# Two chunks prepared ahead of the loop, three Newton operations on VectorE, and expert weights split beside the last chunk

## The reference, cut to what matters

```
def _layernorm(x): m = mean(x); v = var(x); return (x - m) / sqrt(v + 1e-5)
# layer 0 attention: 16 heads of 8, 120 keys per image from ctx_1024
    q = heads(query @ wq_k + wq_b); k, v = heads(ctx @ wk_k + wk_b), heads(ctx @ wv_k + wv_b)
    attn = softmax(q @ k.T / sqrt(8) + neg) * group_prob
    return (attn @ v) @ wo_k + wo_b
# layer 0 experts: top 2 of 8, each with a capacity; gelu(x @ W1[e] + b1[e]) @ W2[e] + b2[e]
# layer 1 attention: the same without group_prob, one mask for all images
# layer 1 experts: every expert for every row, weighted by comb (zero outside the top 2)
    h = x @ W1[e].T + b1[e]; a, b = split(h); out += ((a * sigmoid(b)) @ Wo.T + bo) * comb[e]
x = x + tanh(g_xattn[0]) * attention0(_layernorm(x), ctx);  x = x + tanh(g_ffn[0]) * experts0(_layernorm(x))
x = x + tanh(g_xattn[1]) * attention1(_layernorm(x), ctx);  x = x + tanh(g_ffn[1]) * experts1(_layernorm(x))
```

## Time and profile before

| | us |
|---|---|
| median of 3 runs | 959.44 (957.41 to 962.17) |
| the profiled execution, its own time | 961.64 |
| its span, first to last instruction | 959.8 |
| PE busy | 793.3 (83%) |
| PEld busy | 627.5 (65%) |
| DVE busy | 670.6 (70%) |
| ACT busy | 608.5 (63%) |
| POOL busy | 571.8 (60%) |

### The profile page before, as it was taken

How to read it: one execution, slowest core, us unless ns; L and a number is a source line. 1 busy time by engine, 2 the same in 40 slices (tenths; PEclk the granted TensorE clock), 3 DMA queues, 4 the chain that set the end, 5 groups by cost and what they waited for, 6 DMA issues and landing times.

```text
span 959.8 us, 20423 instructions
## 1 busy us (share of the span) xinstructions
PE 793.3 (83%) x6554; PEld 627.5 (65%) x6554; DVE 670.6 (70%) x1933; ACT 608.5 (63%) x2582; POOL 571.8 (60%) x872
## 2 busy tenths in 40 slices
PE   2268898988886399999876788788986889999996
PEld 1146666766664299998555556656765767888885
DVE  1246889999896534436688799998896575666664
ACT  1366888998982255444787678889996344444442
POOL 6364567888777500223477887574341767777775
PEclk9978999999996699999999889999998899999998
DMA  7929789536633742322537367454300000000000
GB/s 172 243 87 242 197 218 274 138 98 157 128 86 130 259 138 83 85 82 85 110 85 140 72 127 173 112 109 120 89 13 24 22 23 23 21 15 14 8 12 22
DMA packets 83699, 101.68 MB, mean 106 GB/s; under 512 B 8289, under 2 KB 69926, under 8 KB 82665
## 3 DMA queue, kind: packets, MB, share of 16 engines
q1 hardware_dynamic: 79496, 92.13, 37.4%
q0 software_dynamic: 4096, 8.25, 3.5%
HBM read 63.32 MB, written 45.99 MB: 114 GB/s over the span
## 4 chain that ended last, share of the span: by engine, by line
PE 41%; DVE 22%; ACT 14%; POOL 9%; issue 9%; DMA 5%; SPq 0%; POOLq 0%; ACTq 0%; DVEq 0%
ACT exp L805 10%; PE psum L654 7%; PE psum L691 5%; PE psum L693 5%; PE psum L692 5%; DVE shift L986 5%; DVE exp_T L996 2%; PE psum L542 2%; PE psum L529 2%; PE psum L642 2%; DVE ln_stats L968 2%; PE psum L643 2%; PE psum L644 2%; DVE exp_T L998 2%; PE psum L707 1%
## 5 line engine op out<-in xcount | busy, mean ns | idle before, releaser
L805 ACT ACTIVATE exp<-psum,shift 128x120 f32<-128x120 f32 x1024 | 364.8, 427 | 92.9 <-DVE shift L986 92.5
L805 ACT ACTIVATION_READ_ACCUMULATOR exp<-psum,shift 128x1 f32 x1024 | 269.8, 273 | 0.0
L986 DVE TENSOR_REDUCE shift<-psum 128x4 f32<-128x480 f32 x256 | 164.9, 646 | 55.4 <-PE psum L520 54.8
L529 PE MATMUL psum<-ident,exp 128*120 128x128 f32 x1024 | 164.5, 285 | 35.1 <-DVE exp_T L998 22.0
L1569 POOL TENSOR_TENSOR q_operand<-q_operand 128x512 f32<-128x512 f32 x96 | 125.9, 1311 | 70.3 <-DVE q_operand L1345 66.1
L1345 DVE SCALAR_TENSOR_TENSOR q_operand<-psum,comb,q_operand 128x256 f32<-128x256 f32 x256 | 111.7, 479 | 79.9 <-ACT q_operand L933 79.9
L529 PEld LDWEIGHTS psum<-ident,exp 128*120 128x120 f32 x1024 | 120.4, 143 | 53.9 <-DVE exp_T L998 26.5
L933 ACT ACTIVATE q_operand<-psum 128x512 f32<-128x512 f32 x128 | 76.4, 598 | 122.3 <-PE psum L693 122.2
...
L517 PE MATMUL psum<-neg_rows,const_bf 128*128 128x480 bf16 x256 | 98.7, 386 | 48.4 <-ACT exp L805 27.5
L691 PE MATMUL psum<-w_T_high,xn_T_high 128*128 128x512 f32 x256 | 108.8, 425 | 9.5 <-DVE w_T_low L1311 7.3
L693 PE MATMUL psum<-w_T_high,xn_T_low 128*128 128x512 f32 x256 | 102.5, 400 | 0.0
...
...
## 6 DMA issues: line engine op xcount, KB each, us to landing
...
q_operand<-scratch_q SPq DMA_DIRECT2D x30, 384.0 KB, 6.1
scratch_q<-parts SPq DMA_DIRECT2D x15, 384.0 KB
...
scratch_q<-parts SPq DMA_DIRECT2D x15, 256.0 KB
...
```

The lines of the kernel that those rows point to most:

```text
L529: ins = pe.transpose(ps[0:S2, T_BANKS[G % 2], u * S:(u + 1) * S], atts[l].expS[:, G % RING_E, u, :], ident[:, :])
L805: ins = act.activation(atts[l].expS[:, G % RING_E, u, :], ps[:, S_BANKS[G % 3], u * S2:(u + 1) * S2], ACT.Exp, bias=atts[l].shift[:, i % 2 ...
L986: dve.tensor_reduce(atts[l].shift[:, i % 2, 4 * r:4 * r + 4], ps[:, S_BANKS[G % 3], 0:4 * S2].rearrange("p (h k) -> p h k", h=4), AX_X, AL ...
```

## The change

Three things, in one edit.

**Opening.** Layer 0's chunks 0 and 1 (`READY` = 2) are both prepared ahead of the loop, their splits on VectorE (`split`), their norms too; GpSimd keeps the powers, the clearing of the keys' ring, masks and bias. Rows are loaded chunk by chunk, the spare rows of the queries' ring are cleared ring by ring, and the keys of chunk 0 are fetched before its queries' parts go out. Chunk 2 starts at slot 2 instead of 5.

**Newton on VectorE.** For eight norms (`NEWTON_ON_DVE`) the six operations on GpSimd become three on VectorE (`roots`), placed in the slot of the power, so VectorE awaits the power there. Rows are normalised as (x - mean) * r.

**Second experts' weights.** Their halves lie in two buffers of their own, over rings of keys that are done with: five experts (`v_soon`) once chunk 6's scores are through, three (`v_late`) after the last score. The first split stands at slot 117, the rows' at 115; loads start at slot 60 and come every seven. Units 0 and 1 are multiplied up at slots 130 and 133. To make room, GpSimd's gathers for chunks 5 to 7 and chunk 6's bias work are moved by some slots, and three key splits of layer 1 start three slots later.

```diff
-LAST_AT = 64
+LAST_AT, LAST_EVERY = 60, 7
+
+
+SOON_E = 5
+assert (2 * NCH - 1) % RING == 0
+WEIGHTS_AT = [117 + 2 * e for e in range(SOON_E)] + [129 + e for e in range(E - SOON_E)]
+ROWS_AT = 115
 
 ROUTE_STEPS = 26
...
+NEWTON_ON_DVE = [(0, 0), (0, 1), (0, NCH), (0, NCH + 1), (0, NCH + 2), (0, NCH + 3), (1, NCH - 2), (1, NCH - 1)]
+
+
+def newton_on_dve(who, n):
+
+    return (who, n) in NEWTON_ON_DVE
...
-    return ({1: 0, 2: 5, 3: 14} if l == 0 else {1: 0, 2: 0, 3: 0}).get(P, 16 * P - 38)
+    return ({1: 0, 2: 2} if l == 0 else {1: 0, 2: 0, 3: 0}).get(P, 16 * P - 38)
...
+READY = 2
+
+
+def looped(l, P):
+
+    return l == 1 or P >= READY
-    return ({1: NEAR, 2: MID} if l == 0 else {1: NEAR1, 2: MID1, 3: FAR1, 4: FAR2}).get(P, FAR)
+    return ({2: MID} if l == 0 else {1: NEAR1, 2: MID1, 3: FAR1, 4: FAR2}).get(P, FAR)
-    return {8: 0, 9: 7, 10: 9, 11: 11}[i] if c == 2 else {3: 13, 4: 21, 5: 29, 6: 37, 7: 52}[c] + 2 * b
+    return {8: 0, 9: 7, 10: 9, 11: 11}[i] if c == 2 else {3: 13, 4: 21, 5: 30, 6: 45, 7: 60}[c] + 2 * b
...
+TIGHT6 = dict(TIGHT, exp=18, weigh=21, add_bo=22)
+
+
 def post_at(l, j):
-    return POST if j < 5 else TIGHT if l else TIGHT0
+    return POST if j < 5 else TIGHT0 if l == 0 else TIGHT6 if j == NCH - 2 else TIGHT
-SPLIT_KEYS_AT = {2: (0, 1), 5: (2,), 19: (3, 4, 5)}
+SPLIT_KEYS_AT = {5: (0, 1), 8: (2,), 19: (3, 4, 5)}
...
-        vh, vl = sb(mem, "w1_T_high", [D, E, 2 * HID1], F32R), sb(mem, "w1_T_low", [D, E, 2 * HID1], F32R)
+        v_late = sb(mem, "w1_T_split_late", [D, E - SOON_E, 2, 2 * HID1], F32R)
+        gT = sb(mem, "gated_T", [D, 2, HID1])
+        sb(mem, "unused", [D, (PAIRS * 2 * CK * 2 - 8 * HID1 - (E - SOON_E) * 16 * HID1) // 4])
+        v_soon = sb(mem, "w1_T_split_soon", [D, SOON_E, 2, 2 * HID1], F32R)
         xh, xl = sb(mem, "xn_T_high", [D, 2, CT], F32R), sb(mem, "xn_T_low", [D, 2, CT], F32R)
+        total = sb(mem, "gated_sum", [S, 2, HID1])
...
+    def halves(e_):
+
+        both = v_soon[:, e_] if e_ < SOON_E else v_late[:, e_ - SOON_E]
+        return both[:, 0, :], both[:, 1, :]
+
+    def wait_halves_free(on, e_):
+
+        on.wait_ge(score, 16 * (2 * NCH - 1) if e_ < SOON_E else 8 * B)
...
-                project_q(0)
+                for C in range(READY):
+                    project_k(C)
+                    turn_rows(0, C)
+                    project_q(C)
+                if l == 1 and s in units_soon:
+                    ups1(units_soon[s])
...
+            if w == 1:
                 wait_taken(on, 8 * B - 2)
+            if w == 2:
                 wait_taken(on, 8 * B - 1)
                 on.wait_ge(o_T, 2 * B)
...
+        units_soon = {130: 0, 133: 1}
-            if w < UNITS:
+            if w < UNITS and w not in units_soon.values():
...
+                for C in range(READY):
+                    take_projected(1, C)
+                    part0(1, C)
+                    take_turned(0, C)
+                    take_projected(0, C)
+                    part0(0, C)
+                    if C == 0:
+                        make_gates()
+                if l == 1 and s == ROWS_AT:
+                    high_rows(0)
+                if l == 1 and s in WEIGHTS_AT:
+                    high_weights(WEIGHTS_AT.index(s))
+            wait_halves_free(on, e_)
             on.wait_ge(f_less, e_ + 1)
             on.wait_ge(ld_b1, 16 * E)
-            act.copy(vh[:, e_, :], vw[:, e_, :]).then_inc(f_wh, 1)
+            act.copy(halves(e_)[0], vw[:, e_, :]).then_inc(f_wh, 1)
+            on.wait_ge(score, 16 * (2 * NCH - 1))
...
-                high_rows(0)
-                high_weights(0)
-                high_weights(1)
-            if w < PAIRS_E - 1:
-                high_weights(2 * w + 2)
-                high_weights(2 * w + 3)
...
+        def roots(who, n, h=0):
+
+            p = CB // 2 if h else CB
+            r_s, m_v = rs[:, who, :, 0:p], mv[:, who, 0:p, :]
+            power, rstd, m = (h_pow, h_rstd, 0) if h else (ln_pow[who], ln_rstd[who], n)
+            y, t_, r, v = (r_s[:, j, :] for j in (0, 1, 2, 4))
+            on.wait_ge(power, 2 * m + 2)
+            dve.tensor_tensor(t_, y, y, ALU.mult).then_inc(rstd, 1)
+            on.wait_ge(rstd, 6 * m + 1)
+            dve.scalar_tensor_tensor(t_, v, -0.5, t_, ALU.mult, ALU.mult).then_inc(rstd, 1)
+            on.wait_ge(rstd, 6 * m + 2)
+            dve.scalar_tensor_tensor(r, t_, 1.5, y, ALU.add, ALU.mult).then_inc(rstd, 4)
-                dve.tensor_scalar(xn[:, ln_slot(who, n), b, :], x[:, c * CB + b, :], rs[:, who, 2, b:b + 1], rs[:, who, 3, b:b + 1], ALU.mult, ALU.add).then_inc(ln_norm[who], 1)
+                dve.tensor_scalar(xn[:, ln_slot(who, n), b, :], x[:, c * CB + b, :], mv[:, who, b, 0:1], rs[:, who, 2, b:b + 1], ALU.subtract, ALU.mult).then_inc(ln_norm[who], 1)
...
+        def split(k, C):
+            left0(k, C)
+            part1(k, C)
+            left1(k, C)
...
+                    if o == at["power"]:
+                        roots(0, C)
+                if l == 0 and j >= ON_DVE and o == post_at(l, j)["power"]:
+                    roots(1, j)
+                if l == 1 and s == ROWS_AT + 1:
+                    low_rows(0)
+                if l == 1 and s - 1 in WEIGHTS_AT:
+                    low_weights(WEIGHTS_AT.index(s - 1))
+                    roots(0, NCH)
+                    roots(0, HALVED, 1)
...
-            if w == 0:
-                low_rows(0)
-                low_weights(0)
-                low_weights(1)
-            if w < PAIRS_E - 1:
-                low_weights(2 * w + 2)
-                low_weights(2 * w + 3)
...
+        roots(0, 0)
+        normalise_rows(0, 0, 0)
+        split(1, 0)
+        stat_rows(0, 1, 0, 1)
+        split(0, 0)
+        roots(0, 1)
+        normalise_rows(0, 1, 1)
+        split(1, 1)
         on.wait_ge(tanh_done, 2)
         for l in range(2):
             dve.tensor_scalar(bo[:, l, :], bo[:, l, :], tg_x[:, l:l + 1], None, ALU.mult).then_inc(bo_done, 1)
+        split(0, 1)
...
+            if newton_on_dve(who, n):
+                return
         clear_ring(0)
+        powers(0, 0)
+        pool.memset(vx[:], 0.0).then_inc(spread0, 1)
+        powers(0, 1)
         clear_ring(1)
-        pool.memset(vx[:], 0.0).then_inc(spread0, 1)
-        left0(1, 0)
-        part1(1, 0)
-        powers(0, 0)
-        left1(1, 0)
-        normalise_rows(0, 0, 0)
         masks(0)
-        left0(0, 0)
-        part1(0, 0)
-        left1(0, 0)
-        add_bias(0)
+        for C in range(READY):
+            add_bias(C)
...
+        def load_rows(c):
+            if c > 3:
+                wait_rows(on, c - 3)
+            sp.dma_start(x[:, c * CB:(c + 1) * CB, :], t["x"][:, c * CB:(c + 1) * CB, :]).then_inc(ld_rows[c % 3], 16)
+            sp.dma_start(ctxT[:, c * CK:(c + 1) * CK], t["ctxT"][:, c * CK:(c + 1) * CK]).then_inc(ld_rows[c % 3], 16)
...
-            if l == 0 and s == 0:
-                load_rows(1, 2, NCH)
+            for c in range(READY + 1, NCH):
+                if l == 0 and s == 16 * c - 46:
+                    load_rows(c)
...
-        load_rows(0, 1, 2)
-        clear_spares(RING)
+        clear_spares(0, 1)
+        load_rows(1)
         load_masks(0)
         load_group(0)
         for p in range(3):
             parts_out(1, 0, p)
+        fetch_k(0)
         for p in range(3):
             parts_out(0, 0, p)
-        fetch_k(0)
         fetch_q(0)
+        load_rows(2)
+        clear_spares(1, RING)
+        for p in range(3):
+            parts_out(1, 1, p)
+        for p in range(3):
+            parts_out(0, 1, p)
+        fetch_k(1)
+        fetch_q(1)
```

61 lines of the change are left out of this document (30 added, 31 removed).

## The result

The changed kernel takes 948.67 us (median of 4 runs, 945.27 to 948.75), the kernel before 960.81 in the same comparison (4 runs, 957.41 to 962.37): a ratio of 0.9871, interval 0.9837 to 0.9904. That is 12 us faster, where 31 were forecast; 948.67 lies above the range of 916 to 940. The forecast of faster by over 0.5% came true, the size did not.

A forecast was written before the change was run, and what follows sets the result against it. TensorE was taken as full except in the opening, first chunk and 722 to 760 us. Terms -24.3, +1.3, -0.5 and -7.9 sum to -31.4, from the median 959.44 to 928.0; range 916 to 940.

The forecast's parts named there:

- First chunk: Layer 0, slots 0 to 15: stands of TensorE gone, 26.5 us, second chunk starting at 57.5 instead of 81.76.
- Rival (b): Opening's waits only move, chunk 1's operands or chunk 2's rows being late: 10 us of stands, 938 us; chance 0.13.
- First score: Opening of layer 0: first score starts at 31 (bounds 27 and 34), 7.5 us earlier.
- rival (d): Opening has no block, a fetch of 6.2 and a first chunk of 24: 921 us; chance 0.14.
- End of layer 0: Slot 124 on: VectorE stands 4.2 us for a power, chunk 7's norm gains; +1.3 (-2 to +4).
- Front of layer 1: VectorE waits for powers at slots 6, 15, 24, nearly cancelled by GpSimd's earlier gathers: -0.5 (-4 to +4).
- Rival (e): Loops: VectorE's queue stands at each new power until GpSimd gets there, slower than before; chance 0.01.
- Last chunk and second experts: End of layer 1: stands and clock give -11.3, splits on ScalarE cost +3.4; -7.9 (-3 to -11).
- signs of being wrong: First chunk over 35 us, layer 1 power waits over 5 us, or stands around 740 us remaining under other names.

The follow-up runs named there:

- mask_rows_first: The changed kernel with chunk 1's masks and chunk 3's rows loaded ahead of SyncE's fetches of chunk 1's operands; ratio to before 0.9754.
- all_mended: The changed kernel with masks and rows loaded ahead, second ring cleared early, keys behind query parts, gathers in old slots, layer 1's chunks 1-3 Newton on GpSimd; 926.17 us, ratio 0.966.
- ring_early: The changed kernel with GpSimd clearing the second operand ring right behind the first, ahead of the first power; ratio to before 0.9881.
- keys_after: ring_early with chunk 0's keys fetched behind its queries' parts, as in the kernel before; ratio to before 0.9879.
- all_mended_roots0: all_mended with Newton for the second norms of layer 0's chunks 6 and 7 right ahead of their normalising; 922.41 us, ratio 0.9618.
- roots_at_norm: The changed kernel with Newton of layer 1's chunks 1 to 3 on VectorE right ahead of normalising, not in the power's slot; ratio to before 0.9858.
- newton_pool1: The changed kernel with Newton of layer 1's chunks 1 to 3 on GpSimd again, only chunk 0's still on VectorE; ratio to before 0.983.
- weights_late_tight: The changed kernel with second experts' halves made in their first units and chunk 6's layer 1 routing weights and bias work in old slots; ratio to before 0.9968.

## Why the prediction was wrong, step by step

**First chunk (forecast 26.5 us, measured 36.8): the step that failed.** The sentence "what caused the stands is gone from slots 0 to 15" looked at what the change removed and not at what still went through SyncE behind the new fetches. Rival (b) named the form, "the opening's waits only move", with chance 0.13, and dismissed it because the fetches went out 25 us ahead of their slot. The operands were in time indeed, though their fetches went out 10 to 12 us later than forecast; what was late stood behind them: masks, then rows. With these ahead the chunk takes 24.9 us, inside the bounds of 22 and 29.5. Here 10.7 of the 18.5 us were missed. The 3.2 us gained behind it are a separate gain that no term had: the second chunk (slots 16 to 32) takes 27.2 us instead of 30.4 in the changed kernel, and just as much in `mask_rows_first` and `all_mended`, where the first chunk is mended.

**First score (forecast 31, measured 33.24): two parts.** The split of the queries came at 21.07 where 20.1 was said; the block was sized right (2.5 taken, 2.9 measured against `ring_early`). What was missed is again SyncE: the diff puts the keys' fetch ahead of the query parts, and I costed it at nothing. From the end of the split to the fetch of the queries 5.0 us pass instead of the 3.1 said; with the block gone but that order kept it is 8.7 (`ring_early`), with both mended 2.9 (`keys_after`). So it hid the block entirely, and the missing block of rival (d) alone would have gained nothing.

**End of layer 0 (forecast +1.3, measured +0.7): right in the stand, less so in what hides it.** VectorE waits 4.13 us in slot 124 (4.2 said), and chunk 6's norm, shifted by the opening's 14.6 us, comes 2.7 late (2.85 said). But the +1.3 took the stand as nearly hidden before layer 1 starts, and that was too mild: without it layer 1 starts 3.8 us earlier (`all_mended_roots0` against `all_mended`), so something else had paid for it in the changed kernel; what, no run shows. The small miss is luck.

**Front of layer 1 (forecast -0.5, measured +9.1): the second step that failed.** The waits for the powers are there, 1.49, 1.49 and 2.79, 5.8 us together; the third, at slot 24, had no price of its own in the sum. Newton on VectorE cost 7 us in slots 0 to 28, and not the 1.5 to 3 that I took. Some 2.6 to 3.7 of it are these waits, which stand ahead of row maxima (`roots_at_norm`); the rest goes only when the operations leave VectorE too (`newton_pool1`), for a cause that stays open. VectorE is busy for 50.4 of 64 us there, and TensorE's granted clock is 0.87, against 0.97 without. The other side gave back 4.1 between slots 28 and 40. I then went no further. From slot 40 to 88 another 6.2 us were lost (97.3 before, 103.5 after), some 5 of them to the moved gathers of chunks 5 to 7, which stood in the diff and were priced in no term of the sum. Rival (e), a VectorE that stands at every power, had the mechanism; its total did not come about, because the opening's gain remained.

**Last chunk and second experts (forecast -7.9, measured -7.6): right by total, wrong in the cause.** Price 3.4 against 4.2 to 4.3, gain 11.3 against 11.9. But only 6.1 of the gain are the early halves; 4.9 come from chunk 6's bias work, which I had counted in one sum with the halves, and 0.9 is between the kernel before and `weights_late_tight`, for which no run names a cause. With the bias work moved, the early splits gain some 2 us (6.1 - 4.2).

The 11.3 was also made up wrongly, and the errors cancelled, which is luck. Of 10.3 us of stands I kept 0.5; 3.5 are left (0.99 and 2.47), so the stands gave 6.9 and not 9.8. Of the clock I gave back 1.5, having read 0.81 over 38 us as 7 us at the lower level. With levels of 2.4 and 1.2 GHz, a mean of 0.81 over 38 us means 14 us at the lower level, which cost 7 us of full-speed work. In the 45.2 us from slot 127 on the granted clock rose from 0.81 to 0.93; as an estimate this is worth up to 0.12 x 45.2 = 5.4 us:

```profile
719.80:765.00 45.20, 34.09 (x190) 26.72 (x188) 26.46 (x79) 22.40 (x50) 19.78 (x29) 0.81 0.05 16
```

```profile
718.70:763.90 45.20, 41.01 (x249) 32.77 (x250) 30.43 (x103) 25.57 (x56) 27.01 (x35) 0.93 0.07 24
```

Of the prediction's own signs of being wrong, two came: a first chunk of over 35 us, and over 5 us of waits for powers in layer 1. The third, stands around 740 us under other names, came in part.

Faster by over 0.5% was right, by an opening that was worth 14.6 us at slot 124 and is worth 26.6 there in `mask_rows_first` (255.3 against 281.9).
